# Memory stage: the final clips of six heads on POOL, two last-pass clips on DVE, another order

## The chip, the cores and the metric

The kernel runs on one core of a Trainium2 chip. The metric is the time of one execution on the device in microseconds (us), as a median over runs. The engines each have an instruction queue of their own, worked off in order: TensorE (PE) for matrix products, VectorE (DVE), ScalarE (ACT), GpSimd (POOL) and SyncE (SP), which issues transfers. They are tied together by semaphores.

## What is computed

A network of two layers on 4 x 512 rows of 256 numbers. Only the third of its four blocks, an attention over a memory of 256 vectors, is touched. It is repeated three times for each row and each of 8 heads, with entmax weights in place of a softmax:

```python
def entmax15(x):
    x = (x - jnp.max(x, -1, keepdims=True)) / 2.0
    xs = jnp.flip(jnp.sort(x, -1), -1)
    rho = jnp.arange(1, x.shape[-1] + 1, dtype=x.dtype)
    mean = jnp.cumsum(xs, -1) / rho
    meansq = jnp.cumsum(xs * xs, -1) / rho
    ss = rho * (meansq - jnp.square(mean))
    tau = mean - jnp.sqrt(jnp.clip((1.0 - ss) / rho, 0.0, None))
    support = jnp.sum(tau <= xs, -1, keepdims=True)
    tau_star = jnp.take_along_axis(tau, support - 1, -1)
    return jnp.square(jnp.clip(x - tau_star, 0.0, None))
...
for _ in range(NUM_STEPS):
    scores = jnp.einsum('bhsd,hnd->bhsn', xi, K) * beta
    w = entmax15(scores)
    xi = jnp.einsum('bhsn,hnd->bhsd', w, V)
out = xi.transpose(0, 2, 1, 3).reshape(B, S, H * hd) @ Wo.T
```

and then `x = x + layernorm(out)`.

## The kernel before

The rows stand in 16 tiles of 128 (one row per partition). A tile goes through three steps, so there are 48 units of work (`Unit`). Four tiles are in flight as four lanes: unit m is in lane m mod 4, and unit m+4 is the next step of the same tile, so its scores need the weights of unit m. The weight matrices are multiplied together beforehand into G1, G2 and G3.

A unit passes through these steps, each a small function of `memory_block`:

- PE: `score`, 16 matmuls into four PSUM banks (two heads, a pair, in each). The banks are shared by all units: pair p of a unit may be written once the first clip of that pair of the unit before has read it.
- DVE: `largest`, the eight largest scores of each head, eight instructions.
- A start value for the threshold: POOL `centre`, `square`, three `running_sum`, `mean_and_gap`, `mean_square`, `add_gap`, `add_room`; DVE `clear`; ACT `bound_root`; POOL `step_back`; DVE `bound`; POOL `start`, which writes `shift`. Each waits for the one before.
- Four Newton passes k = 0 to 3: ACT `clip`, relu(u + shift) for each of 8 heads, from PSUM into `u` in pass 0 and in place after that; DVE `take_moments`, one instruction per pair; DVE `invert`; POOL `second_moment`; ACT `newton_root`; POOL `newton`, which writes the next `shift`.
- `weights`, the final clip of each head with the last `shift`: before, all eight on DVE (line 1208).
- PE `transpose` (two heads at a time, with a warming matmul ahead), ACT `columns`, which squares the transposed weights into `wT`; after the third step PE `output`, DVE `out_stats`, POOL `out_rstd`, DVE `out_norm`.
- For the first step of a tile also DVE `tile_stats`, POOL `tile_rstd`, DVE `tile_rows`, PE `tile_transpose`, ACT `tile_columns`.

The `u` of three lanes lies in `mem_arena`, that of the fourth in `r_u`; rows of both names are the same work.

The order is written by hand for each engine as the body of a loop over slots n: a list of calls, each for the unit `Unit(n - something)`. One round of the loop, a slot, does one unit's worth of work on each engine, taken from several units at different steps. A call for a unit that isn't live issues nothing. Output and tile steps occur in 16 of the slots each; a slot with neither is called plain here.

Of the kernel before, what the change touches and what calls it, by code (L numbers as in the profile page):

```python
# [1046 lines left out]
DVE_HEADS = (0, 1, 2, 3, 4, 5, 6, 7)  # L1047
ACT_HEADS = ()
FIRST_SLOT, LAST_SLOT = -3, TILES * STEPS - 1 + 9
# [18 lines left out]
def memory_block(nc, T):  # L1068
    X, ident, vec, G1, G2, G3 = (T[n] for n in ("X", "ident", "vec", "G1", "G2", "G3"))
    col = lambda name, k: vec[:, VEC[name][0] + k:VEC[name][0] + k + 1]  # L1070
    with ExitStack() as ctx:
# [3 lines left out]
        def sem(name):  # L1075
# [49 lines left out]
        clipped, moments_ready, inv_ready, s2_ready, root_ready, shift_ready = (  # L1125
            [sem(f"{n}{k}") for k in range(PASSES)] for n in (
                "clipped", "moments_ready", "inv_ready", "s2_ready", "root_ready", "shift_ready"))
        dve_weights, act_weights, wT_in_psum, wT_ready = (sem(n) for n in (
            "dve_weights", "act_weights", "wT_in_psum", "wT_ready"))
# [16 lines left out]
        def _(dve):  # L1146
# [39 lines left out]

            def take_moments(a, k, *pairs):
                if not a.live:
                    return
                for p in pairs:  # L1190
                    dve.wait_ge(clipped[k], of_unit(a, NPAIR, p + 1))
                    last = dve.bn_stats(moments[:, a.lane, 2 * p:2 * p + 2, :].rearrange("p two c -> p (two c)"),  # L1192
                                        u[a.lane][:, 2 * p:2 * p + 2, :].rearrange("p two n -> p n two"))
                    if p == NPAIR - 1:
                        last.then_inc(moments_ready[k], 1)
# [29 lines left out]
            for n in range(FIRST_SLOT, LAST_SLOT + 1):  # L1225
                invert(Unit(n - 8), 3)
                largest(Unit(n - 5), 2)
                invert(Unit(n - 6), 0)
                largest(Unit(n - 5), 3)
                take_moments(Unit(n - 7), 2, 2, 3)  # L1230
                largest(Unit(n - 5), 4)
                weights(Unit(n - 8), 0)
                invert(Unit(n - 7), 2)
                largest(Unit(n - 5), 5, 6, 7)
                weights(Unit(n - 8), 1)
                take_moments(Unit(n - 6), 1, 0)
                weights(Unit(n - 8), 2)
                take_moments(Unit(n - 6), 1, 1, 2)
                take_moments(Unit(n - 7), 3, 0)
                weights(Unit(n - 8), 3)  # L1240
                take_moments(Unit(n - 6), 1, 3)
                take_moments(Unit(n - 7), 3, 1)
                clear(Unit(n - 5))
                weights(Unit(n - 8), 4, 5)
                invert(Unit(n - 6), 1)
                tile_rows(Unit(n - 2))
                take_moments(Unit(n - 7), 3, 2)
                bound(Unit(n - 5))
                weights(Unit(n - 8), 6, 7)
                take_moments(Unit(n - 7), 3, 3)  # L1250
                out_stats(Unit(n - 9))
                tile_stats(Unit(n + 3))
                take_moments(Unit(n - 6), 2, 0)
                take_moments(Unit(n - 5), 0, 0, 1, 2)
                out_norm(Unit(n - 9))
                take_moments(Unit(n - 5), 0, 3)
                take_moments(Unit(n - 6), 2, 1)
                largest(Unit(n - 4), 0, 1)

        @block.gpsimd  # L1260
        def _(pool):
# [100 lines left out]

            def out_rstd(a):
# [7 lines left out]
            for n in range(FIRST_SLOT, LAST_SLOT + 1):  # L1371
                running_sum(Unit(n - 5), 2)
                mean_and_gap(Unit(n - 5))
                mean_square(Unit(n - 5))
                add_gap(Unit(n - 5))
                add_room(Unit(n - 5))
                second_moment(Unit(n - 6), 1)
                step_back(Unit(n - 5))
                newton(Unit(n - 6), 1)
                start(Unit(n - 5))  # L1380
                out_rstd(Unit(n - 9))
                second_moment(Unit(n - 5), 0)
                tile_rstd(Unit(n - 1))
                second_moment(Unit(n - 7), 3)
                newton(Unit(n - 5), 0)
                newton(Unit(n - 7), 3)
                second_moment(Unit(n - 6), 2)
                newton(Unit(n - 6), 2)
                centre(Unit(n - 4))
                square(Unit(n - 4))  # L1390
                running_sum(Unit(n - 4), 0)
                running_sum(Unit(n - 4), 1)

        @block.scalar
        def _(act):
# [37 lines left out]
            def weights(a, *heads):  # L1433
                if not a.live:
                    return
                act.wait_ge(shift_ready[PASSES - 1], of_unit(a))
                for h in heads:
                    act.activation(u[a.lane][:, h, :], u[a.lane][:, h, :], ACT.Relu,
                                   bias=shift[:, a.lane, h:h + 1]).then_inc(act_weights, 1)

# [9 lines left out]
            for n in range(FIRST_SLOT, LAST_SLOT + 1):  # L1450
                clip(Unit(n - 3), 2, 0, 1)
                clip(Unit(n - 2), 0, 0, 1, 2, 3, 4, 5, 6, 7)
                clip(Unit(n - 3), 2, 2, 3)
                columns(Unit(n - 5), 2)
                clip(Unit(n - 3), 2, 4, 5)
                columns(Unit(n - 5), 3)
                newton_root(Unit(n - 2), 0)
                clip(Unit(n - 3), 2, 6, 7)
                newton_root(Unit(n - 4), 3)
                clip(Unit(n - 2), 1, 0, 1, 2)  # L1460
                tile_columns(Unit(n - 0))
                newton_root(Unit(n - 3), 2)
                clip(Unit(n - 2), 1, 3)
# [1134 lines left out]
```

## Time and profile before

| | us |
|---|---|
| median of 3 runs | 1927.84 |
| lowest, highest | 1927.65, 1935.23 |
| the profiled execution | 1928.65 |
| its span, first to last instruction | 1926.9 |

| engine | busy us | share of the span |
|---|---|---|
| PE, matmuls | 1657.8 | 86% |
| DVE | 1383.7 | 72% |
| ACT | 1166.3 | 61% |
| POOL | 611.3 | 32% |

The shares are means over stages. The page's strip of 40 slices shows the memory stage as the stretch in which DVE and ACT are at nine tenths or more, slices 12 to 27; POOL stands at four or five tenths there. Durations in rows run from the start of an instruction to its end; consecutive instructions of an engine overlap, so that what one costs its queue is the distance from its start to the next start.

### The profile page before, as it was taken

The numbers are of one execution on the slowest core, as the hardware profiler recorded it, in microseconds if no ns is written. First come the engines' busy times: TensorE is split into PE (matmuls) and PEld (weight loads), VectorE is DVE, ScalarE is ACT, GpSimd is POOL, SyncE is SP. The second block draws the span as 40 slices with busy tenths as digits, with TensorE's granted clock in tenths as the row PEclk, the third lists the DMA queues.
The fourth block names the chain that finished last, engine by engine and source line by source line (L and its number), as shares of the span: only waits on it lengthen the run. The fifth ranks groups of instructions, "written<-read, shape, count | busy, mean of one in ns | idle before, by whom it ended". The sixth has DMA issues, their size and how long they took to land. (4 is left out here: it accounts for less than half of the span.)

```text
span 1926.9 us, 26070 instructions
## 1 busy us (share of the span) xinstructions
PE 1657.8 (86%) x7634; PEld 1153.4 (60%) x7634; DVE 1383.7 (72%) x3597; ACT 1166.3 (61%) x2844; POOL 611.3 (32%) x1916
## 2 busy tenths in 40 slices
PE   5899999989657889988998789887688999999987
PEld 2545656465545667766786678665545556555554
DVE  6565747562359999999999999999444475665646
ACT  3242333311249999999999999999247364564640
POOL 3504224140034455545544555444210101002000
PEclk9698989998878889988998899889899999999989
DMA  5000000000300000000000000000000000000000
GB/s 217 1 1 1 1 1 1 0 1 1 118 1 1 1 1 1 1 1 1 1 1 1 1 1 1 1 1 1 1 1 1 1 2 1 1 12 0 8 6 22
DMA packets 6862, 19.90 MB, mean 10 GB/s; under 512 B 960, under 2 KB 3904, under 8 KB 5440
## 3 DMA queue, kind: packets, MB, share of 16 engines
q1 hardware_dynamic: 6720, 18.23, 2.5%
q8 instruction: 62, 1.02, 0.2%
q14 instruction: 80, 0.66, 0.1%
HBM read 16.13 MB, written 2.10 MB: 9 GB/s over the span
## 5 line engine op out<-in xcount | busy, mean ns | idle before, releaser
L1422 ACT ACTIVATE mem_arena<-mem_arena,r_shift 128x256 f32<-128x256 f32 x864 | 385.0, 510 | 23.1 <-POOL r_shift L1361 23.0
L1192 DVE BATCH_NORM_STATS2 r_moments<-mem_arena 128x6 f32<-128x512 f32 x576 | 380.4, 690 | 10.6 <-ACT mem_arena L1422 7.5
L1501 PE MATMUL r_bank<-G,r_wT 128*128 128x256 f32 x1024 | 234.7, 388 | 3.8 <-ACT mem_arena L1422 3.0
L1501 PEld LDWEIGHTS r_bank<-G,r_wT 128*128 128x128 f32 x1024 | 197.2, 196 | 35.1 <-issue 8.3
L1517 PE MATMUL r_bank<-ident,mem_arena 128*128 128x128 f32 x576 | 113.2, 330 | 73.2 <-DVE mem_arena L1208 73.1
L2047 ACT ACTIVATE e_rows_p<-e_seen,e_NM 128x512 f32<-128x512 f32 (+3 forms) x256 | 134.3, 557 | 64.1 <-DVE e_NM L1739 64.1
L1169 DVE MAX8 r_top<-r_bank 128x8 f32<-128x256 f32 x384 | 145.6, 406 | 19.4 <-PE r_bank L1501 19.0
L1511 PE MATMUL r_bank<-G,ident 128*128 128x256 f32 x384 | 143.6, 461 | 9.9 <-ACT r_wT L1448 9.7
L1517 PEld LDWEIGHTS r_bank<-ident,mem_arena 128*128 128x128 f32 x576 | 82.5, 169 | 115.8 <-DVE mem_arena L1208 106.7
L1501 PE MATMUL r_bank<-G,r_xnT 128*128 128x256 f32 x512 | 120.9, 397 | 24.4 <-ACT mem_arena L1422 23.7
L1739 DVE CUSTOM_DVE_ANT_0 e_seen<-e_banks,mask_q 128x512 f32<-128x512 f32 (+3 forms) x256 | 110.4, 486 | 43.3 <-PE e_banks L2250 42.2
L1192 DVE BATCH_NORM_STATS2 r_moments<-r_u 128x6 f32<-128x512 f32 x192 | 129.7, 691 | 8.9 <-ACT r_u L1422 8.2
L1422 ACT ACTIVATE r_u<-r_u,r_shift 128x256 f32<-128x256 f32 x288 | 131.8, 510 | 5.1 <-POOL r_shift L1361 5.1
L2058 ACT ACTIVATE mem_arena<-e_banks 128x512 f32<-128x512 f32 x160 | 92.4, 591 | 61.9 <-PE e_banks L2269 61.6
L1448 ACT ACTIVATE r_wT<-r_bank 128x512 f32<-128x512 f32 x192 | 116.6, 607 | 19.0 <-PE r_bank L1517 19.0
L1501 PEld LDWEIGHTS r_bank<-G,r_xnT 128*128 128x128 f32 x512 | 101.3, 201 | 40.3 <-issue 25.8
L1530 PE MATMUL r_bank<-G,r_wT 128*128 128x256 f32 x512 | 120.0, 384 | 4.8 <-DVE X L1223 4.8
L1422 ACT ACTIVATE mem_arena<-r_bank,r_shift 128x256 f32<-128x256 f32 x288 | 108.2, 483 | 1.3 <-POOL r_shift L1343 1.3
L1349 POOL TENSOR_TENSOR r_spread<-r_moments,r_inv_n 128x8 f32<-128x8 f32 x192 | 39.3, 205 | 212.1 <-DVE r_moments L1192 210.0
L1530 PEld LDWEIGHTS r_bank<-G,r_wT 128*128 128x128 f32 x512 | 95.8, 192 | 17.3 <-ACT r_wT L1448 5.4
L2269 PEld LDWEIGHTS e_banks<-ident,e_rows_p 128*128 128x128 f32 x640 | 74.2, 141 | 49.6 <-issue 25.0
L2269 PE MATMUL e_banks<-ident,e_rows_p 128*128 128x128 f32 x640 | 91.4, 274 | 6.8 <-ACT e_rows_p L2047 4.6
(295 smaller groups left out, 3308.2 us busy)
## 6 DMA issues: line engine op xcount, KB each, us to landing
w<-in_w SPq DMA_DIRECT2D x3, 1024.0 KB, 14.6
out_x<-X SPq DMA_DIRECT2D x4, 512.0 KB, 2.9
X<-in_x SPq DMA_DIRECT2D x1, 1536.0 KB, 10.8
w_in<-in_w_in SPq DMA_DIRECT2D x1, 1156.0 KB, 6.5
mem_arena<-in_wq SPq DMA_DIRECT2D x1, 1024.0 KB, 17.0
mem_arena<-in_wo SPq DMA_DIRECT2D x1, 1024.0 KB, 20.9
gate<-in_gate SPq DMA_DIRECT2D x1, 1024.0 KB, 6.5
up<-in_up SPq DMA_DIRECT2D x1, 1024.0 KB, 8.5
```

The lines of the kernel that those rows point to most:

```text
L1169: last = dve.max(top[:, a.lane, h, :], scores[:, h, :])
L1192: last = dve.bn_stats(moments[:, a.lane, 2 * p:2 * p + 2, :].rearrange("p two c -> p (two c)"), u[a.lane][:, 2 * p:2 * p + 2, :].rearrange ...
L1422: last = act.activation(u[a.lane][:, h, :], u[a.lane][:, h, :] if k else scores[:, h, :], ACT.Relu, bias=shift[:, a.lane, h:h + 1])
L1448: act.activation(wT[:, a.lane, 2 * p:2 * p + 2, :, :], bank[:, TB + p % 2, :], ACT.Square).then_inc(wT_ready, 1)
L1501: last = pe.matmul(scores[:, h, :], lhs, (G1 if a.first else G2)[:, h, i, :], start=i == 0, stop=i == 1)
L1511: pe.matmul(bank[:, TB + p % 2, 0:NMEM], ident[:], G1[:, 0, 0, :], start=True, stop=True)
L1517: last = pe.transpose(bank[:, TB + p % 2, i * P:(i + 1) * P], u[a.lane][:, h, piece * P:(piece + 1) * P], ident[:])
L1530: last = pe.matmul(bank[:, OUT, 0:D], wT[:, a.lane, h, piece, :], G3[:, h, piece, :], start=h == 0 and piece == 0, stop=h == NHM - 1 and p ...
L1739: last = dve.tensor_tensor_reduce(out=seen[:, j, c0:c0 + width], in0=bank[LOOK + j][:, c0:c0 + width], in1=T["mask_q"][:, S - width:], sca ...
L2047: last = act.activation(rows_p[:, j, P_AT[i]:P_AT[i] + width], seen[:, j, c0:c0 + width], ACT.Exp, scale=-1.0, bias=NM[:, i, j:j + 1])
L2058: act.activation(PT[kb][:, :, (i - kb) * P:(i - kb + 1) * P], bank[t_bank(a, g, r)].rearrange("p (j q) -> p j q", j=4), ACT.Copy).then_inc ...
L2269: last = pe.transpose(o[:, j * P:(j + 1) * P], rows_p[:, j, P_AT[i] + kb * P:P_AT[i] + (kb + 1) * P], ident[:])
```

## The change

`weights` of heads 2 to 7 moves from DVE to POOL, as a tensor_scalar with the same two operations; heads 0 and 1 stay on DVE. In the last pass (k = 3) the clips of heads 6 and 7 (pair 3) move from ACT to DVE, through a new function `clip` on DVE. PE waits for both sources of weights. The order lists of all four engines are rewritten, of which two lines stand here, and the loop begins two slots earlier.

```diff
-DVE_HEADS = (0, 1, 2, 3, 4, 5, 6, 7)
-ACT_HEADS = ()
-FIRST_SLOT, LAST_SLOT = -3, TILES * STEPS - 1 + 9
+DVE_HEADS = (0, 1)
+POOL_HEADS = (2, 3, 4, 5, 6, 7)
+DVE_CLIPS = ((), (), (), (3,))
+FIRST_SLOT, LAST_SLOT = -5, TILES * STEPS - 1 + 9
...
+            def clip(a, k, *heads):
+                if not a.live:
+                    return
+                dve.wait_ge(shift_ready[k - 1], of_unit(a))
+                for h in heads:
+                    last = dve.tensor_scalar(u[a.lane][:, h, :], u[a.lane][:, h, :], shift[:, a.lane, h:h + 1], 0.0,
+                                             ALU.add, ALU.max)
+                    if h % 2:
+                        last.then_inc(dve_clipped[k], 1)
...
                 for p in pairs:
-                    dve.wait_ge(clipped[k], of_unit(a, NPAIR, p + 1))
+                    if p in DVE_CLIPS[k]:
+                        dve.wait_ge(dve_clipped[k], of_unit(a, len(DVE_CLIPS[k]), DVE_CLIPS[k].index(p) + 1))
+                    else:
+                        dve.wait_ge(clipped[k], of_unit(a, NPAIR - len(DVE_CLIPS[k]), p + 1 - sum(q < p for q in DVE_CLIPS[k])))
...
+            def weights(a, *heads):
+                if not a.live:
+                    return
+                pool.wait_ge(shift_ready[PASSES - 1], of_unit(a))
+                for h in heads:
+                    pool.tensor_scalar(u[a.lane][:, h, :], u[a.lane][:, h, :], shift[:, a.lane, h:h + 1], 0.0, ALU.add,
+                                       ALU.max).then_inc(pool_weights, 1)
...
-                centre(Unit(n - 4))
-                square(Unit(n - 4))
+                centre(Unit(n + 2))
+                square(Unit(n + 2))
+                newton(Unit(n - 0), 2)
...
-                    pe.wait_ge(dve_weights, of_unit(a, len(DVE_HEADS), sum(h <= 2 * p + 1 for h in DVE_HEADS)))
-                    if any(h // 2 == p for h in ACT_HEADS):
-                        pe.wait_ge(act_weights, of_unit(a, len(ACT_HEADS), sum(h <= 2 * p + 1 for h in ACT_HEADS)))
+                    if any(h // 2 == p for h in DVE_HEADS):
+                        pe.wait_ge(dve_weights, of_unit(a, len(DVE_HEADS), sum(h <= 2 * p + 1 for h in DVE_HEADS)))
+                    if any(h // 2 == p for h in POOL_HEADS):
+                        pe.wait_ge(pool_weights, of_unit(a, len(POOL_HEADS), sum(h <= 2 * p + 1 for h in POOL_HEADS)))
```

DVE in the middle of the stage, before, from a unit's last three `largest` (MAX) through `clear` (TENSOR_SCALAR r_room) to the first instruction of its `bound`; L1192 is a moment, L1208 a weight clip, L1201 `invert`:

```order
L1169 MAX r_top<-r_bank 128x8 x3
L1208 TENSOR_SCALAR mem_arena<-mem_arena,r_shift 128x256
L1192 BN_STATS r_moments<-mem_arena 128x6
L1208 TENSOR_SCALAR mem_arena<-mem_arena,r_shift 128x256
L1192 BN_STATS r_moments<-mem_arena 128x6 x3
L1208 TENSOR_SCALAR mem_arena<-mem_arena,r_shift 128x256
L1192 BN_STATS r_moments<-mem_arena 128x6 x2
L1177 TENSOR_SCALAR r_room<-r_room 128x64
L1208 TENSOR_SCALAR mem_arena<-mem_arena,r_shift 128x256 x2
L1201 RECIPROCAL r_inv<-r_moments 128x8
L1192 BN_STATS r_moments<-mem_arena 128x6
L1183 TENSOR_TENSOR r_back<-r_back,r_fold 128x64
```

The same stretch of DVE in the changed kernel, in a plain slot too; L1206 is a moment, L1222 a weight clip, L1193 the new clip of the last pass:

```order
L1170 MAX r_top<-r_bank 128x8 x3
L1222 TENSOR_SCALAR r_u<-r_u,r_shift 128x256
L1215 RECIPROCAL r_inv<-r_moments 128x8
L1206 BN_STATS r_moments<-mem_arena 128x6
L1222 TENSOR_SCALAR r_u<-r_u,r_shift 128x256
L1206 BN_STATS r_moments<-mem_arena 128x6 x4
L1178 TENSOR_SCALAR r_room<-r_room 128x64
L1193 TENSOR_SCALAR mem_arena<-mem_arena,r_shift 128x256
L1206 BN_STATS r_moments<-mem_arena 128x6
L1184 TENSOR_TENSOR r_back<-r_back,r_fold 128x64
```

Between the last `largest` and `clear` there stand five moments, two weight clips and a reciprocal where there stood six moments and three weight clips; behind `clear` one weight clip and `invert` fewer.

POOL before, from a second moment and `newton` (L1358, L1361) to the three running sums (L1304), `centre` being L1287 and `square` L1295:

```order
L1349 TENSOR_TENSOR r_spread<-r_moments,r_inv_n 128x8
L1350 TENSOR_TENSOR r_meansq<-r_moments 128x8
L1352 TENSOR_TENSOR r_s<-r_spread,r_meansq 128x8
L1358 TENSOR_TENSOR r_spread<-r_root,r_s 128x8
L1361 TENSOR_TENSOR r_shift<-r_spread,r_inv 128x8
L1287 TENSOR_TENSOR r_fold<-r_top 128x8x8
L1295 TENSOR_TENSOR r_fold<-r_fold 128x8x8
L1304 TENSOR_TENSOR r_fold<-r_fold 128x16x8 x3
```

POOL in the changed kernel at the same place, from its fourth weight clip (L1381) on; L1371 and L1374 are `newton`, L1300 is `centre`, L1308 `square`, L1317 the sums:

```order
L1381 TENSOR_SCALAR r_u<-r_u,r_shift 128x256
L1371 TENSOR_TENSOR r_spread<-r_root,r_s 128x8
L1374 TENSOR_TENSOR r_shift<-r_spread,r_inv 128x8
L1381 TENSOR_SCALAR r_u<-r_u,r_shift 128x256 x2
L1362 TENSOR_TENSOR r_spread<-r_moments,r_inv_n 128x8
L1363 TENSOR_TENSOR r_meansq<-r_moments 128x8
L1365 TENSOR_TENSOR r_s<-r_spread,r_meansq 128x8
L1300 TENSOR_TENSOR r_fold<-r_top 128x8x8
L1308 TENSOR_TENSOR r_fold<-r_fold 128x8x8
L1371 TENSOR_TENSOR r_spread<-r_root,r_s 128x8
L1374 TENSOR_TENSOR r_shift<-r_spread,r_inv 128x8
L1317 TENSOR_TENSOR r_fold<-r_fold 128x16x8 x3
```

Weight clips now stand ahead of `centre`, and the `newton` of pass 2 stands between `square` and the sums.

## Rows read from the trace of the kernel before

**Rows 1.** Windows: stretch, us; busy (instructions) of PE, PEld, DVE, ACT, POOL; clock, DMA.

```profile
800.00:900.00 100.00, 82.03 (x357) 65.09 (x356) 97.01 (x251) 93.20 (x250) 50.07 (x200) 0.87 0.00 1
```

**Rows 2.** One line's instructions, `start`: duration least/median/most, first and last start.

```profile
L1343 POOL TENSOR_TENSOR r_shift<-r_neg,r_top x48: 208/246/248, 550.7 to 1330.8; 128x8 f32<-128x8 f32 x48
```

**Rows 3.** Groups by line, 700 to 1300 us: busy, mean ns, idle before, releaser.

```profile
L1422 ACT ACTIVATE mem_arena<-mem_arena,r_shift 128x256 f32<-128x256 f32 x650 | 290.1, 510 | 12.8 <-POOL r_shift L1361 12.7
...
L1349 POOL TENSOR_TENSOR r_spread<-r_moments,r_inv_n 128x8 f32<-128x8 f32 x144 | 29.4, 204 | 152.2 <-DVE r_moments L1192 150.7
...
L1221 DVE TENSOR_SCALAR r_onorm<-r_bank,r_omv,r_ors 128x256 f32<-128x256 f32 x12 | 6.4, 531 | 0.0
...
L1223 DVE TENSOR_TENSOR X<-X,r_onorm 128x256 f32<-128x256 f32 x12 | 5.1, 425 | 0.9
```

**Rows 4.** Timeline of DVE, 1077 to 1099 us: start, duration, instruction.

```profile
1081.85 0.18 DVE L1177 TENSOR_SCALAR r_room<-r_room 128x64 f32<-128x64 f32 x1
...
1083.15 0.20 DVE L1183 TENSOR_TENSOR r_back<-r_back,r_fold 128x64 f32<-128x64 f32 x1
...
1083.57 0.61 DVE L1208 TENSOR_SCALAR mem_arena<-mem_arena,r_shift 128x256 f32<-128x256 f32 x2
1084.09 0.69 DVE L1192 BATCH_NORM_STATS2 r_moments<-mem_arena 128x6 f32<-128x512 f32 x1
1084.70 0.69 DVE L1192 BATCH_NORM_STATS2 r_moments<-r_u 128x6 f32<-128x512 f32 x1
...
1089.40 0.18 DVE L1201 RECIPROCAL r_inv<-r_moments 128x8 f32<-128x8 f32 x1
1089.50 0.38 DVE L1169 MAX8 r_top<-r_bank 128x8 f32<-128x256 f32 x1
...
1092.10 1.14 DVE L1169 MAX8 r_top<-r_bank 128x8 f32<-128x256 f32 x3
1093.16 0.34 DVE L1208 TENSOR_SCALAR mem_arena<-mem_arena,r_shift 128x256 f32<-128x256 f32 x1
...
1096.33 0.34 DVE L1208 TENSOR_SCALAR mem_arena<-mem_arena,r_shift 128x256 f32<-128x256 f32 x1
```

**Rows 5.** Timeline of POOL over the same stretch.

```profile
1077.51 0.33 POOL L1287 TENSOR_TENSOR r_fold<-r_top 128x64 f32<-128x64 f32 x1
...
1081.34 0.32 POOL L1331 TENSOR_TENSOR r_room<-r_room,r_inv_k 128x64 f32<-128x64 f32 x1
1081.62 0.20 POOL L1349 TENSOR_TENSOR r_spread<-r_moments,r_inv_n 128x8 f32<-128x8 f32 x1
...
1082.12 0.23 POOL L1352 TENSOR_TENSOR r_s<-r_spread,r_meansq 128x8 f32<-128x8 f32 x1
...
1082.62 0.32 POOL L1337 TENSOR_TENSOR r_back<-r_mean,r_room 128x64 f32<-128x64 f32 x1 [0.27 <-ACT r_room L1412]
...
1091.12 0.20 POOL L1358 TENSOR_TENSOR r_spread<-r_root,r_s 128x8 f32<-128x8 f32 x1
1091.46 0.20 POOL L1361 TENSOR_TENSOR r_shift<-r_spread,r_inv 128x8 f32<-128x8 f32 x1
...
1093.32 0.32 POOL L1287 TENSOR_TENSOR r_fold<-r_top 128x64 f32<-128x64 f32 x1
...
1096.35 0.47 POOL L1319 TENSOR_TENSOR r_back<-r_mean 128x64 f32<-128x64 f32 x1
1096.89 0.32 POOL L1325 TENSOR_TENSOR r_room<-r_room,r_back 128x64 f32<-128x64 f32 x1
```

**Rows 6.** Groups by line and shape of POOL, whole span; columns as in rows 3.

```profile
L1304 POOL TENSOR_TENSOR r_fold<-r_fold 128x128 f32<-128x128 f32 x144 | 63.5, 441 | 11.3
...
L504 POOL TENSOR_TENSOR m_xd<-m_xt,m_dt 128x512 f32<-128x512 f32 x16 | 16.6, 1039 | 131.3 <-ACT m_xt L633 131.3
...
L1369 POOL TENSOR_TENSOR r_ors<-r_ove,half_neg 128x1 f32<-128x1 f32 x16 | 8.8, 549 | 2.6 <-issue 0.4
...
L1269 POOL MEMSET r_fold<- 128x256 f32 x3 | 0.8, 311 | 0.0
```

## What the change does to the time: the prediction

> **What bounds the kernel now.** I read the windows first: of 100 us of the memory stage DVE is busy 97.01 us, ACT 93.20, PE 82.03 and POOL 50.07 [rows 1]. So DVE is the bound, ACT follows closely, and POOL has room. The start instruction of the 48 units, one each, runs from 550.7 to 1330.8 us [rows 2]: 780.1 us over 47 intervals, 16.60 us per unit. The groups by line show that POOL's largest idle time is before the second moment: 152.2 us before 144 of them, four per unit, so 4.2 us per unit in which POOL waits for DVE's moments [rows 3].
>
> DVE's and POOL's timelines price the loop [rows 4, 5]. A slot without tile work runs from one `centre` at 1077.51 to the next at 1093.32: 15.81 us. It has two halves. In the first POOL makes the sums (last add 1081.34), DVE clears (1081.85), ACT takes the root, POOL steps back (1082.62) and DVE makes the bound (1083.15): 5.64 us. In the second DVE works through its queue from the bound to the end of the eighth `largest` (1092.10 plus 1.06, next instruction at 1093.16), and `centre` follows 0.16 us later: 10.17 us. In the first half DVE is never idle today, since moments and weights fill it; the loop and DVE's own load come out alike.
>
> **The change, engine by engine.** *DVE* loses six weight clips per unit and gains two clips of the last pass. Two clips took 0.52 us from start to next start (1083.57 to 1084.09), 0.26 each, so four fewer save 1.04 us. Its steady load falls from 97.01% of 16.60, 16.10, to 15.06 us. *ACT* loses two clips of 510 ns [rows 3]; from start to start they cost somewhat less, I take 0.4, so 0.8 us: from 15.5 to 14.7 us. *POOL* gains six tensor_scalar of 128x256. If nothing but load counted, a unit would take 15.06 plus today's 0.50 of DVE idle, 15.56 us, and the saving would be 1.04 times 48, 50 us.
>
> *The order.* It moves all four moments of pass 0 and of pass 2 ahead of the eighth `largest`, and leaves little between that and the clear. From the rows a moment costs 0.61 (1084.09 to 1084.70), a `largest` 0.35 (1.06 for three), a reciprocal 0.10 (1089.40 to 1089.50), the bound 0.42. Second half of the loop after the change: bound 0.42, one clip 0.26, ten moments 6.10, three reciprocals 0.30, eight `largest` 2.80, and 0.16 to `centre`: 10.04 us. The same sum for before (nine moments, three clips) is 9.95, against 10.17 in the trace. So this half is not shortened at all: one moment came in and two clips went.
>
> In the first half POOL's chain of sums cannot be hidden. Today it takes 3.83 us from `centre` to the last add. The new order puts a `newton` of pass 2 behind `square`: 0.34 (1091.12 to 1091.46) plus 0.16, of which about 0.1 hides in the wait for the square, so plus 0.4. DVE meanwhile has two weight clips, one reciprocal and five moments, 3.67 us, while the last add starts 0.16 plus 3.83 plus 0.4, 4.39 us, after the last `largest`, and its result comes 0.4 later. DVE will sit idle about 1.1 us in front of `clear` in every slot without tile work. What is queued behind: the clip of head 6, the moments and the bound, for which the next unit's first clips on ACT wait. Then clear 0.10, clip 0.26 and a moment 0.61 stand before the bound, 0.97 us, against 1.30 seen from clear to bound today. First half: 3.83 less some 0.1 (below), plus 0.4, plus 0.4 to the clear, plus 1.0: 5.5 us. The lower bound is 5.1 (the newton hidden whole), the upper 6.04 (3.83, 0.4, and the 0.51 and 1.30 of the trace), with the 0.22 by which the trace lay above my sum for the second half. Plain slot: 15.55 us, between 15.1 and 16.3, against 15.81 now. Where the last `largest` ends later than its load says, for a score that PE has late, that would add as well; PE's matmuls come in bursts with 18% idle [rows 1], and I count none.
>
> *Slots with tile work.* 16 of 48 slots hold an output norm. Its statistics and norm on DVE now lie in the idle stretch, but `out_rstd` on POOL stands before `add_gap`, and DVE's norm before `clear`. Counted from the last `largest`: POOL reaches `out_rstd` at 3.99 (the last add's 4.39 less one 0.40), takes 0.34 to its power (as from 1091.12 to 1091.46) and 0.55 for it [rows 6], then DVE's two norm instructions take 0.96 [rows 3]; with 0.1 for the hand-over the clear starts at 5.94 and not 4.79, 1.15 us later than in a plain slot. Tile statistics and rows, three instructions, become free. The tile's two columns on ACT stand just before the last-pass clip that DVE's moments wait for; I put this at 0.3 us in 16 slots. Mean: 15.55 + 1.15/3 + 0.3/3 = 16.03 us. Today's mean lies 0.79 above its plain slot, so part of the gain comes here.
>
> *POOL's clip.* No such instruction is in the trace. Nearest rows: a memset of the same 128x256 takes 311 ns, a tensor_tensor of 128x128 441, one of 128x512 1039 [rows 6]; on the line between these two 128x256 is 640. One input and one output lie between memset and tensor_tensor; I take 0.45, bounds 0.31 and 0.64, and as a further end 1.04, if halving the row saved nothing. POOL's budget between pass 3's moments and the next `centre` is the 7.8 us that DVE needs for eight moments, eight `largest` and one reciprocal. In it: three second moments of 0.66 (1081.62 to 1082.12, plus 0.16), two newtons of 0.5, a wait of some 0.9 for ACT's root, and six clips: 3.9 + 6w. It fits up to w = 0.65, just over my upper bound. At 0.45 all six are free.
>
> By the Trainium skill (GPSIMD Engine Reference, section 4.1) an elementwise instruction with one input runs there roughly at line rate, and its section 1 gives 1.2 GHz. Estimated from that page, 256 elements take 0.21 us, with the trace's 0.2 us for the smallest instructions some 0.42 us; the sum would stay what it is.
>
> *Contention.* Where a DVE clip began at 1096.33, POOL's 128x64 product took 0.47 us, and the next came 0.54 later rather than 0.40 [rows 5]: 0.14 us per meeting. The new order has two such clips in POOL's chain and not five, my 0.1 above; POOL's own clips meet DVE's moments and `largest` only. The Trainium skill (SBUF — State Buffer, section Who interferes with whom) says that a VectorE tensor_scalar in a two-port mode and a GpSimd instruction exclude each other for their whole length, and whichever starts later waits. By that rule a DVE clip that falls on a POOL clip would wait up to 0.45 us, with four per unit at most 1.8; by the order they don't meet.
>
> **Rivals.**
> 1. *Load alone decides*: DVE's idle is filled because `centre` or the sums come out earlier than I think. 15.56 us, 50 us saved, 1878. For it: DVE at 97%. Against it: the second half of the loop is DVE's own work and the first is serial.
> 2. *The upper ends hold*: plain slot 15.9 to 16.3, from ACT late at roots (it waits for `shift` of pass 2, now made after `square`) and more meetings. With 0.48 for tile work the mean is 16.4 to 16.8, and the time 1919 to 1937: no change that can be measured.
> 3. *POOL's clip is dear* (slower): above 0.65 us each clip delays `centre`, six times the excess per slot. It eats my 0.57 us at w = 0.75. At 0.9, near the middle of 0.64 and 1.04, the slot is 16.03 + 6 x 0.25 = 17.53 and the time 1928.65 + 47 x 0.93 = 1972. Against it: the one row with fewer than two inputs, the memset, lies at 0.31.
> The Trainium skill (GPSIMD Engine Reference, section 3.1) speaks against the change as a whole: "use DVE for elementwise". An estimate from the 2.6 cycles per element that it gives for two inputs is 0.55 us, with the trace's 0.2 for the smallest instructions 0.75, at which the change would bring nothing; no row here shows which rate holds for this form.
>
> **The numbers.** The sum is made on the profiled execution, 1928.65 us with a span of 1926.9; the median is 0.8 lower. 47 x (16.60 - 16.03) = 26.8 us; I let the filling and draining of the pipeline stand. 1928.65 - 26.8 - 0.8 = 1901; with a little for waits that no row shows, 1903. Chances: forecast (1890 to 1917) 0.5; load alone (below 1890) 0.14; upper ends 0.21; dear clip 0.15. For 8 in 10 the range goes from 1876 to 1936, with the forecast's own 1890 to 1917. A measurement of this kernel can tell 0.5%, 9.6 us, from no change. Faster by that: 0.65; within: 0.20; slower: 0.15.
>
> **What the new profile would show.** POOL tensor_scalar of 0.35 to 0.6 us; DVE idle about 1 us before `clear` in plain slots, ended by POOL; DVE busy 93 to 94% in the stage; starts about 16.0 apart. I am wrong if the clip is above 0.65 us, or if `clear` has no wait before it, or if ACT, which now idles 6.8 of 100 us [rows 1], shows over 12.

## The result

The changed kernel takes 2025.72 us (median of 4 runs, 2024.04 to 2030.28), before 1927.74 in the same comparison: ratio 1.050, interval 1.047 to 1.053. It is slower by 98 us where 25 us less were forecast.

All of it lies in the memory stage. The same row as in [rows 2] is, of the kernel after:

```profile
L1356 POOL TENSOR_TENSOR r_shift<-r_neg,r_top x48: 207/242/246, 551.0 to 1429.5; 128x8 f32<-128x8 f32 x48
```

878.5 us over 47 intervals make 18.69 us per unit, against 16.60 before. 47 times the difference is 98 us.

The windows of after, with the columns of [rows 1], show who is busy now:

```profile
800.00:900.00 100.00, 73.54 (x349) 61.04 (x347) 85.25 (x205) 79.49 (x210) 79.10 (x211) 0.93 0.00 1
```

DVE fell from 97 to 85, ACT from 93 to 79, and POOL rose from 50 to 79, so that no engine looks full. The reason is in two rows for POOL's new clip, of the view of one line's instructions (duration least/median/most):

```profile
L1381 POOL TENSOR_SCALAR mem_arena<-mem_arena,r_shift x216: 1134/1139/1247, 588.8 to 1455.8; 128x256 f32<-128x256 f32 x108
L1381 POOL TENSOR_SCALAR r_u<-r_u,r_shift x72: 1136/1139/1298, 643.2 to 1470.9; 128x256 f32<-128x256 f32 x72
```

1139 ns per head, where I had taken 450 and bounded at 640, with 1040 as a far end. Six of them are 6.8 us, added to POOL's serial work. POOL's timeline in one slot of after shows how they fill it up to `centre` (L1300):

```profile
1002.29 3.38 POOL L1381 TENSOR_SCALAR mem_arena<-mem_arena,r_shift 128x256 f32<-128x256 f32 x3
1005.64 0.20 POOL L1362 TENSOR_TENSOR r_spread<-r_moments,r_inv_n 128x8 f32<-128x8 f32 x1
...
1006.32 1.14 POOL L1381 TENSOR_SCALAR mem_arena<-mem_arena,r_shift 128x256 f32<-128x256 f32 x1
...
1007.95 2.36 POOL L1381 TENSOR_SCALAR mem_arena<-mem_arena,r_shift 128x256 f32<-128x256 f32 x2
1010.28 0.23 POOL L1362 TENSOR_TENSOR r_spread<-r_moments,r_inv_n 128x8 f32<-128x8 f32 x1
...
1010.97 0.29 POOL L1300 TENSOR_TENSOR r_fold<-r_top 128x64 f32<-128x64 f32 x1
```

The last two clips end at 1010.31. The second moment behind them starts without a wait, its moments being long there, and `centre` follows it without a wait, though DVE made its last `largest` of the unit by 1009.1 (1008.03 plus 1.08). From start to start a clip takes 1.12 us (3.38 less 1.14, halved).

Who waits for POOL, from the list of waits of after, 700 to 1300 us (total, times, longest):

```profile
ACT r_root L1455 <- POOL r_s L1365: 91.2, 64, 3.2
...
DVE r_moments L1206 <- ACT mem_arena L1446: 44.9, 84, 1.5
POOL r_spread L1362 <- DVE r_moments L1206: 30.9, 32, 1.6
```

ACT waits at the root for a second moment that stands in POOL's queue behind clips, for about 2.8 us per unit, and DVE waits for ACT's clips in turn. POOL's own wait for moments, 152 us in [rows 3], is down to 31.

### The profile page after: what moved, and what is told of

It is laid out like the page before. It is cut to its first block and busy times, and to the rows that moved or that the text cites. A ratio compares the mean times of both kernels' runs of the same rounds, so it can differ in the third digit from the quotient of the medians.

```text
span 2025.6 us, 26072 instructions
## 1 busy us (share of the span) xinstructions
PE 1669.5 (82%) x7634; PEld 1171.7 (58%) x7634; DVE 1358.1 (67%) x3405; ACT 1134.3 (56%) x2748; POOL 917.6 (45%) x2204
## 5 line engine op out<-in xcount | busy, mean ns | idle before, releaser
L1206 DVE BATCH_NORM_STATS2 r_moments<-mem_arena 128x6 f32<-128x512 f32 x576 | 386.1, 686 | 70.7 <-ACT mem_arena L1446 68.0
L1446 ACT ACTIVATE mem_arena<-mem_arena,r_shift 128x256 f32<-128x256 f32 x792 | 356.4, 506 | 26.6 <-POOL r_shift L1374 22.8
L1381 POOL TENSOR_SCALAR mem_arena<-mem_arena,r_shift 128x256 f32<-128x256 f32 x216 | 247.0, 1155 | 3.5
L1517 PEld LDWEIGHTS r_bank<-G,r_wT 128*128 128x128 f32 x1024 | 199.3, 198 | 54.4 <-ACT r_wT L1464 18.6
L1534 PEld LDWEIGHTS r_bank<-ident,mem_arena 128*128 128x128 f32 x576 | 93.2, 179 | 103.1 <-DVE mem_arena L1222 82.3
L1206 DVE BATCH_NORM_STATS2 r_moments<-r_u 128x6 f32<-128x512 f32 x192 | 129.7, 686 | 30.2 <-ACT r_u L1446 29.2
L1527 PEld LDWEIGHTS r_bank<-G,ident 128*128 128x128 f32 x384 | 74.8, 231 | 104.0 <-ACT r_wT L1464 101.4
L1446 ACT ACTIVATE r_u<-r_u,r_shift 128x256 f32<-128x256 f32 x264 | 120.2, 507 | 9.8 <-POOL r_shift L1374 8.5
L1455 ACT ACTIVATE r_root<-r_s 128x8 f32<-128x8 f32 x192 | 40.0, 208 | 142.5 <-POOL r_s L1365 142.5
L1446 ACT ACTIVATE mem_arena<-r_bank,r_shift 128x256 f32<-128x256 f32 x288 | 117.1, 490 | 1.3 <-POOL r_shift L1356 1.1
L1464 ACT ACTIVATE r_wT<-r_bank 128x512 f32<-128x512 f32 x192 | 108.9, 591 | 10.6 <-PE r_bank L1534 10.6
```

The source lines that it names most:

```text
L1381: pool.tensor_scalar(u[a.lane][:, h, :], u[a.lane][:, h, :], shift[:, a.lane, h:h + 1], 0.0, ALU.add, ALU.max).then_inc(pool_weights, 1)
L1446: last = act.activation(u[a.lane][:, h, :], u[a.lane][:, h, :] if k else scores[:, h, :], ACT.Relu, bias=shift[:, a.lane, h:h + 1])
L1464: act.activation(wT[:, a.lane, 2 * p:2 * p + 2, :, :], bank[:, TB + p % 2, :], ACT.Square).then_inc(wT_ready, 1)
L1517: last = pe.matmul(scores[:, h, :], lhs, (G1 if a.first else G2)[:, h, i, :], start=i == 0, stop=i == 1)
L1527: pe.matmul(bank[:, TB + p % 2, 0:NMEM], ident[:], G1[:, 0, 0, :], start=True, stop=True)
L1534: last = pe.transpose(bank[:, TB + p % 2, i * P:(i + 1) * P], u[a.lane][:, h, piece * P:(piece + 1) * P], ident[:])
```

## The experiments

**Theory A**: POOL's clip is dear by itself and pushes POOL's queue over a threshold of some 0.65 us per clip. **Theory B**: the new order costs the time, whatever a clip takes. **Theory C**: the clip is long only since it meets DVE's work.

### What POOL's forms cost alone

```diff
+            for n in (8, 64, 128, 256, 512):
+                four(n, lambda o, x: pool.tensor_scalar(o, x, col[:, 0:1], 0.0, ALU.add, ALU.max))
+            for n in (8, 256):
+                four(n, lambda o, x: pool.tensor_scalar(o, x, col[:, 0:1], None, ALU.add))
+            four(256, lambda o, x: pool.tensor_scalar(o, x, 1.0, 0.0, ALU.add, ALU.max))
+            four(256, lambda o, x: pool.tensor_scalar(o, x, 0.0, None, ALU.max))
+            four(256, lambda o, x: pool.tensor_copy(o, x))
+            four(256, lambda o, x: pool.tensor_tensor(o, x, src[:, 256:512], ALU.add))
+            four(256, lambda o, x: pool.tensor_tensor(o, x, col[:, 0:1].to_broadcast([P, 256]), ALU.add))
```

> The kernel before, with a stretch of its own between the memory and the experts stage in which POOL alone works, on scratch tiles: four each of tensor_scalar add+max with a per-partition scalar at 8, 64, 128, 256 and 512 columns, add alone at 8 and 256, add+max with constants at 256, max alone, copy, tensor_tensor and tensor_tensor with a broadcast column at 256. Theory A (the clip is dear by itself, per element): 1.1 us at 256, about 0.2 at 8, a straight line between, so some 0.67 at 128 and 2.1 at 512. Theory C (it is long since it meets DVE's work): under 0.7 at 256 with DVE silent. Whether the two operations or the per-partition scalar make the price is open; if each operation is a pass, add alone takes about 0.65. Time some 30 us over before.

The groups by line and shape of POOL (busy, mean ns of one):

```profile
L1566 POOL TENSOR_SCALAR q_dst<-q_src,q_col 128x512 f32<-128x512 f32 x4 | 7.9, 1992 | 0.2 <-issue 0.2
L1566 POOL TENSOR_SCALAR q_dst<-q_src,q_col 128x256 f32<-128x256 f32 x4 | 4.5, 1138 | 0.2 <-issue 0.2
L1569 POOL TENSOR_SCALAR q_dst<-q_src 128x256 f32<-128x256 f32 x4 | 4.2, 1066 | 0.2 <-issue 0.2
L1568 POOL TENSOR_SCALAR q_dst<-q_src,q_col 128x256 f32<-128x256 f32 x4 | 3.6, 928 | 0.2 <-issue 0.2
L1570 POOL TENSOR_SCALAR q_dst<-q_src 128x256 f32<-128x256 f32 x4 | 3.3, 846 | 0.2 <-issue 0.2
L1566 POOL TENSOR_SCALAR q_dst<-q_src,q_col 128x128 f32<-128x128 f32 x4 | 2.8, 712 | 0.2 <-issue 0.2
L1572 POOL TENSOR_TENSOR q_dst<-q_src 128x256 f32<-128x256 f32 x4 | 2.8, 722 | 0.1
L1573 POOL TENSOR_TENSOR q_dst<-q_src,q_col 128x256 f32<-128x256 f32 x4 | 2.3, 612 | 0.1
...
L1571 POOL COPY q_dst<-q_src 128x256 f32<-128x256 f32 x4 | 1.4, 398 | 0.1
L1566 POOL TENSOR_SCALAR q_dst<-q_src,q_col 128x8 f32<-128x8 f32 x4 | 1.2, 324 | 0.3 <-issue 0.3
```

The run, a single one, took 1973.45 us, 43 more than before beside it, for the stretch added, in which no other engine has an instruction. There the clip takes 1138 ns, as in the stage: theory C has fallen. It costs about 0.3 us plus 3.3 ns per column (1992 less 1138 over 256). It isn't two passes: the add alone takes 928, the max alone 846. It isn't the per-partition scalar: constants in its place take 1066. What is dear is the form. A tensor_tensor of the same size with its two inputs takes 722, and with the column broadcast 612. So the interpolation between tensor_tensor rows in my prediction, as a value for tensor_tensor, was fair (640 against 722); it was no bound for tensor_scalar. The Trainium skill (GPSIMD Engine Reference, section 4.1) gives one-input instructions as roughly line rate; the copy agrees with that (398 ns, where the estimate in the prediction was some 0.42 us), and no tensor_scalar of 256 columns here does: 846 at least.

### The changed kernel with a cheaper clip

```diff
-                    pool.tensor_scalar(u[a.lane][:, h, :], u[a.lane][:, h, :], shift[:, a.lane, h:h + 1], 0.0, ALU.add,
+                    pool.tensor_scalar(u[a.lane][:, h, 0:128], u[a.lane][:, h, 0:128], shift[:, a.lane, h:h + 1], 0.0, ALU.add,
```

> The changed kernel, but POOL clips only 128 of the 256 columns of each of its heads (the other half of the final clip is left out). Theory A (the price of POOL's clip, threshold 0.65 us): the clip takes about 0.67 us, slot 16.0 to 16.3, time 1900 to 1915. Theory B (the new order costs the time, whatever the clip takes): 1990 or more.

and the same with `0:64`:

> As the one with half the columns, but 64 of 256. Theory A: clip about 0.43 us, under the threshold with room, so POOL has slack and the time is that of the forecast, 1895 to 1910, hardly below the half-column run. Theory B: 1990 or more. If time falls in proportion to columns from the changed kernel through both, there is no threshold and my layout of POOL's budget is wrong.

| POOL's clips | ns of one | us, median | ratio to before | us per unit |
|---|---|---|---|---|
| six of 256 columns (the change) | 1139 | 2025.72 | 1.050 | 18.69 |
| six of 128 | 712 | 1914.04 | 0.992 (0.989 to 0.995) | 16.46 |
| six of 64 | 499 | 1908.56 | 0.990 (0.986 to 0.994) | 16.19 |

The column of units is the better measure: the memory stage is reached at 545.4 us (first `centre`) in the trace of the change, at 544.5 with 128 columns and at 553.9 with 64, through code that all three share. In 47 intervals 427 ns less bring 105 us, and the next 213 ns bring 13. That is a threshold, and theory B has fallen as the cause. Plain slots show it best, as the distance of two `centre` in POOL's timeline. The kernel after, then the one with 64 columns:

```profile
878.29 0.29 POOL L1300 TENSOR_TENSOR r_fold<-r_top 128x64 f32<-128x64 f32 x1
896.35 0.29 POOL L1300 TENSOR_TENSOR r_fold<-r_top 128x64 f32<-128x64 f32 x1
```

```profile
848.95 0.32 POOL L1300 TENSOR_TENSOR r_fold<-r_top 128x64 f32<-128x64 f32 x1 [0.40 <-DVE r_top L1170]
864.32 0.33 POOL L1300 TENSOR_TENSOR r_fold<-r_top 128x64 f32<-128x64 f32 x1 [0.29 <-DVE r_top L1170]
```

18.06 and 15.37 us. Under the threshold `centre` waits for DVE's `largest`; above it, it waits for nothing but its own queue. The difference divided by six clips is 0.45, so the threshold lies at 1.12 less 0.45, 0.67 us. Other plain slots of after take up to 18.28, which gives 0.63. With 128 columns, 0.69 us from start to start, the plain slots are at 15.69 and `centre` again has no wait: 0.32 us over six clips put the threshold at 0.64.

One thing moved beside the clips. The granted clock of TensorE from 700 to 1300 us is 0.92 before, 0.89 in after, and 0.98 and 0.99 in the two runs with cut clips. What part of the two runs' gain over before (0.8% and 1.0%) that is, no run separates; the threshold does not rest on it, since the plain slots end on DVE or on POOL.

### The order with all clips on DVE

```diff
-DVE_HEADS = (0, 1)
-POOL_HEADS = (2, 3, 4, 5, 6, 7)
+DVE_HEADS = (0, 1, 2, 3, 4, 5, 6, 7)
+POOL_HEADS = ()
...
-                weights(Unit(n - 8), 0)
+                weights(Unit(n - 8), 0, 1, 2, 3)
...
-                weights(Unit(n - 8), 1)
+                weights(Unit(n - 8), 4, 5, 6, 7)
```

> The changed kernel's order, but all eight final clips on DVE, heads 0 to 3 where head 0 stood and 4 to 7 where head 1 stood; POOL has none. Theory A: the six clips of 0.26 us go partly into DVE's idle 1.1 us before clear, slot 16.4 to 16.8, time 1918 to 1940, as before. Theory B: 1990 or more.

2024.59 us, ratio 1.051 (1.046 to 1.056): a miss for theory A as I had worked it out. With POOL free of clips the time is that of the change, for another reason. PE stands in the waits of this run, 700 to 1300 us:

```profile
POOL r_spread L1362 <- DVE r_moments L1206: 185.5, 114, 3.4
ACT r_room L1433 <- DVE r_room L1178: 51.0, 31, 2.5
...
DVE r_top L1170 <- PE r_bank L1514: 28.2, 38, 1.5
```

POOL waits for DVE, and DVE for scores and for its own longer queue before `clear`. As means over the units from 700 to 1300 us, `clear` starts 6.6 us behind `centre`, where it is 4.8 in the run with 64 columns, and from the bound to the end of the last `largest` it takes 11.2 us instead of 10.4. So about two thirds of the loss is DVE's own queue: I had counted on an idle time of 1.1 us there, six more clips need 1.56, and they take longer than 0.26 each beside POOL's sums. Here four of them take 1.43 us up to the next instruction at 867.54, though POOL has no clip in this run:

```profile
866.11 1.51 DVE L1222 TENSOR_SCALAR mem_arena<-mem_arena,r_shift 128x256 f32<-128x256 f32 x4
```

Most of the rest is waiting for scores, 0.9 us per unit against 0.1: PE must transpose a unit's eight heads before it makes the scores of four units on, so late clips lengthen a second loop, through PE. To test that, six of the eight clips were put ahead of the last three `largest` and two behind:

```diff
                 largest(Unit(n - 5), 2)
+                weights(Unit(n - 8), 0, 1)
...
                 largest(Unit(n - 5), 3)
+                weights(Unit(n - 8), 2, 3)
...
                 largest(Unit(n - 5), 4)
+                weights(Unit(n - 8), 4, 5)
...
                 largest(Unit(n - 5), 5, 6, 7)
-                weights(Unit(n - 8), 0)
+                weights(Unit(n - 8), 6, 7)
```

> All eight final clips on DVE in the new order, as in the run with heads 4 to 7 late, but six of them before the last largest and two right behind it, so that PE's transposes and with them its scores are not late. By the loop from bound to the last largest: six clips of 0.26 us are added to it, slot 16.2 + 1.6 = 17.8, time 1970 to 1985. If late transposes were not what made the other run slow, this one is at 2020 again.

1988.07 us, ratio 1.030 (1.025 to 1.035), 37 us less than the run with late clips and 3 us above the range given. It doesn't single out PE: the wait for scores fell by 0.5 us per unit, but `clear` is also back at 4.9 us behind `centre`, 1.7 less, and from the bound to the last `largest` it takes 1.0 more. Its plain slots:

```profile
887.36 0.32 POOL L1302 TENSOR_TENSOR r_fold<-r_top 128x64 f32<-128x64 f32 x1 [0.29 <-DVE r_top L1170]
904.44 0.33 POOL L1302 TENSOR_TENSOR r_fold<-r_top 128x64 f32<-128x64 f32 x1 [0.29 <-DVE r_top L1170]
```

17.08 us, 1.71 above the 15.37 with cheap clips on POOL, for six clips of 0.26 in the loop (1.56). So the order is fitted to clips that POOL makes; without them it is worse than the order before.

### Fewer heads on POOL

With four heads on POOL (4 to 7), 0 and 1 behind the last `largest`, 2 and 3 where head 1 stood:

```diff
-DVE_HEADS = (0, 1)
-POOL_HEADS = (2, 3, 4, 5, 6, 7)
+DVE_HEADS = (0, 1, 2, 3)
+POOL_HEADS = (4, 5, 6, 7)
...
-                weights(Unit(n - 8), 0)
+                weights(Unit(n - 8), 0, 1)
...
-                weights(Unit(n - 8), 1)
+                weights(Unit(n - 8), 2, 3)
```

> As the one with three, with four heads on POOL (4 to 7). By the threshold 3.9 + 4 x 1.12 = 8.4, 0.6 us over, slot 16.8, time 1928 to 1945. If the time falls evenly with the number of heads from the changed kernel's 2026: two heads fewer would be a third of the way to the forecast, 1985.

1941.58 us, ratio 1.006 (1.004 to 1.009), inside what the threshold gives and far from an even share per head; its ten runs spread from 1935 to 1954. Most plain slots are at 15.96, 0.59 over 15.37, and `centre` has no wait there: four clips of 1.12 are 0.6 too many, as 3.9 + 4w against 7.8 has it. With three heads, 5 to 7, and five on DVE (0, 1 and then 2, 3, 4 in the same two places):

> The changed kernel with three heads on POOL (5, 6, 7) and five on DVE. By the threshold: 3.9 + 3 x 1.12 = 7.3 us, under the 7.8 that DVE needs, so POOL is off the loop; the three clips more on DVE lie in its idle time before clear: slot 16.2 to 16.5, time 1908 to 1922. If the order is what costs: over 1960.

1964.67 us, ratio 1.017 (1.013 to 1.021): a miss. POOL was under its threshold (`centre` waits for `largest` again), but the clips don't fit in DVE's idle time before `clear`: it starts 5.5 us behind `centre`, 0.7 later than with 64 columns, and DVE's wait for scores grew by 0.3. In its list of waits ACT is idle for `clear`, and PE's scores wait for ACT's first clips, which free the banks:

```profile
PE r_bank L1516 <- ACT mem_arena L1445: 34.7, 17, 2.7
...
ACT r_room L1435 <- DVE r_room L1178: 28.2, 30, 2.1
```

Both were tried again with DVE's clips earlier. Four on POOL, 0 and 1 ahead of the last three `largest`, 2 and 3 behind them:

```diff
+                weights(Unit(n - 8), 0, 1)
                 largest(Unit(n - 5), 5, 6, 7)
-                weights(Unit(n - 8), 0)
+                weights(Unit(n - 8), 2, 3)
...
-                weights(Unit(n - 8), 1)
```

> The changed kernel with four heads on POOL (4 to 7) and four on DVE, heads 0 and 1 in front of the last three largest, 2 and 3 right behind them. Against the run with four heads and later clips (slots 16.0 to 18.8, 1942 us): POOL gets 0.5 us more room before centre, PE can transpose 0.6 us sooner. By the two-loop theory (POOL's budget in plain slots, PE's transposes, output and scores in output slots): plain 15.9 to 16.0, output slots 17.2 to 17.6, mean 16.4, time 1912 to 1928, so perhaps just below the kernel before. If PE has no part in it: 1938 to 1945 as there.

and three on POOL, 0 to 2 ahead and 3, 4 behind:

> The same with three heads on POOL (5 to 7), heads 0 to 2 in front of the last three largest, 3 and 4 behind. Two-loop theory: plain 15.38 + 3 x 0.26 = 16.2, output slots 17.3 to 17.7, time 1918 to 1932, against 1965 for the run with three heads and late clips. If the number of heads on POOL alone decided: 1965 again, or less than the run with four.

1951.86 us (ratio 1.011, 1.009 to 1.013) and 1960.90 (1.017, 1.014 to 1.019): two misses. With four heads some plain slots were as given, at 15.9 to 16.0, and others at 17.1 to 17.3. Once in twelve units DVE waits for scores for 3.4 to 3.6 us, which this row of its timeline shows in that run:

```profile
740.82 0.43 DVE L1170 MAX8 r_top<-r_bank 128x8 f32<-128x256 f32 x1 [3.36 <-PE r_bank L1517]
```

PE's timeline ahead of it, and the window of 732 to 736 us (columns as in [rows 1]):

```profile
726.42 0.60 PE L1527 MATMUL r_bank<-G,ident 128*128 128x256 f32 x2
...
730.81 1.22 PE L1527 MATMUL r_bank<-G,ident 128*128 128x256 f32 x2 [2.46 <-ACT r_wT L1464]
731.82 1.06 PE L1534 MATMUL r_bank<-ident,mem_arena 128*128 128x128 f32 x4
...
734.38 4.67 PE L1547 MATMUL r_bank<-G,r_wT 128*128 128x256 f32 x16
```

```profile
732.00:736.00 4.00, 4.00 (x15) 3.44 (x14) 3.49 (x9) 3.93 (x13) 1.75 (x9) 0.50 0.01 2
```

In the middle of the transposes PE waits 2.46 us for ACT's `columns` to free a bank, and behind that its granted clock is 0.50, the lower of its two levels (1.2 GHz). The warming matmul, 0.60 us before, takes 1.22, and the first half of the output 4.67 where the run with 64 columns has 3.62. The other two waits of over 3 us have the same wait of 2.46 and the same 0.50 ahead of them. Earlier weights on DVE thus let PE run into ACT's queue: it waits for `columns` for 58 and 66 us of 600 in these two runs, for 39 and 26 in those with later clips. `columns` earlier on ACT wasn't tried. No version of the new order with whole clips was faster than before.

### Two clips on POOL in the order before

```diff
-DVE_HEADS = (0, 1, 2, 3, 4, 5, 6, 7)
+DVE_HEADS = (0, 1, 2, 3, 4, 5)
+POOL_HEADS = (6, 7)
...
-                weights(Unit(n - 8), 6, 7)
...
                 start(Unit(n - 5))
+                weights(Unit(n - 8), 6, 7)
```

> The kernel before in its own order, with one thing moved: the final clips of heads 6 and 7 go from DVE (right behind bound) to POOL (right behind start), where POOL waits 4.4 us for moments. Two clips of 1.12 us fit in that wait, DVE loses 0.52 us per unit. If load on DVE decides there: up to 25 us saved, 1903 to 1918. Rival: the two clips end 2 us later, PE has the transposes of pair 3 in front of all scores of the next unit, and the scores then come late for DVE's largest: no gain or a loss, 1925 to 1960.

1979.45 us, ratio 1.024 (1.021 to 1.028), slower even than its rival gave. PE waits for the two clips, and DVE for the scores behind them:

```profile
DVE r_top L1170 <- PE r_bank L1502: 42.4, 50, 2.3
...
PEld r_bank L1519 <- POOL mem_arena L1368: 39.6, 22, 2.8
```

DVE's wait for scores is 1.3 us per unit where it was 0.1. POOL was idle at that place for 4 us, and yet the move costs 50 us: idle time on the engine that takes work over is not enough, the result has a reader.

### The last pass's clips back on ACT

```diff
-DVE_CLIPS = ((), (), (), (3,))
+DVE_CLIPS = ((), (), (), ())
...
-                clip(Unit(n - 7), 3, 6)
...
-                clip(Unit(n - 7), 3, 7)
...
-                clip(Unit(n - 5), 3, 5)
+                clip(Unit(n - 5), 3, 5, 6, 7)
```

> The changed kernel with the last pass's clips of heads 6 and 7 back on ACT, right behind head 5. Theory A (POOL's clips are the loop): 0.52 us less on DVE and 0.8 more on ACT change nothing, 2020 to 2035. If ACT was the second loop: over 2045.

2056.13 us, ratio 1.066 (1.062 to 1.069), 30 more than the change, and a miss for theory A, which had ACT out of the loop. 24 of the 30 us lie in the 47 intervals (19.20 us per unit against 18.69). POOL's queue holds a `newton` that waits for ACT's root, and this wait has grown; the changed kernel first, then this run, 700 to 1300 us:

```profile
POOL r_spread L1371 <- ACT r_root L1455: 14.1, 20, 0.8
```

```profile
POOL r_spread L1369 <- ACT r_root L1453: 28.3, 30, 1.4
```

14 us in some 32 units, 0.45 each; over 48 units that is 21 of the 24 us. Beside six clips on POOL this half of the change, DVE taking a pair of clips, is worth having; it was the other half that lost. What it brings without them no run shows.

### The output slots

In the run with 64 columns plain slots are at 15.4, but most of those with an output norm at 17.5. My forecast had 1.15 us for them. To see PE's share, half of the output product was left out there, pairs 0 and 1, which stand before the next scores:

```diff
-                    for i in range(4):
+                    for i in range(4 if p > 1 else 0):
                         h, piece = 2 * p + i // KN, i % KN
                         last = pe.matmul(bank[:, OUT, 0:D], wT[:, a.lane, h, piece, :], G3[:, h, piece, :],
-                                         start=h == 0 and piece == 0, stop=h == NHM - 1 and piece == KN - 1)
+                                         start=h == 4 and piece == 0, stop=h == NHM - 1 and piece == KN - 1)
```

> The run with a quarter of the columns, and of the output product only pairs 2 and 3 (PE's 16 half-matmuls of pairs 0 and 1, 3.6 us in front of the next scores, are left out). Theory PE (in output slots the next unit's scores wait behind output): the slots of 17.5 us fall to 16.3 to 16.8, time 1885 to 1895. Theory of my forecast (out_rstd and the norm before clear alone set the output slot): they stay at 17.5, time 1905 to 1912.

1893.44 us, 15 less, in the range of theory PE, but by luck. The slots of 17.5 fell only to 17.2, not to 16.3 to 16.8, and of the 15.5 us between the spans of the two profiled executions only 4.6 lie in the 47 intervals (16.09 us per unit against 16.19); the memory stage began 5.5 us earlier, and from the last `centre` to the end it took 5.5 less. So 3.6 us of PE's work are worth 0.35 us of an output slot, and theory PE fell as it stood. In the run with 64 columns, DVE just ahead of an output slot, and POOL in it:

```profile
937.07 0.43 DVE L1170 MAX8 r_top<-r_bank 128x8 f32<-128x256 f32 x1 [0.80 <-PE r_bank L1517]
```

```profile
943.09 0.32 POOL L1300 TENSOR_TENSOR r_fold<-r_top 128x64 f32<-128x64 f32 x1 [0.38 <-DVE r_top L1170]
...
947.10 0.56 POOL L1390 TENSOR_TENSOR r_ors<-r_ove,half_neg 128x1 f32<-128x1 f32 x1
```

DVE's norm starts at 947.70, 4.6 us after `centre`, and its two instructions keep `clear` back to 948.71, 5.62 us after `centre`, where a plain slot has 4.4: 1.2, the 1.15 us of the prediction. Three output slots from 700 to 1300 us have no tile columns on ACT in them. Two take 16.51 and 16.43 us, about 1.1 over the plain slot; the third takes 18.09, and 16.52 with half the output product left out, so that it is PE's. The slots at 17.5 all have those columns, for which I had 0.3 us; they cost 1.0 there. In the slot shown DVE waits 0.25 and 0.22 us for ACT's clips behind them, and 0.35 of the 1.0 went with half the output product. The slot before this one has columns and no norm and takes 17.12; the 0.80 before a `largest` is in it.

## Why the prediction was wrong

**The step that failed** is "One input and one output lie between memset and tensor_tensor; I take 0.45, bounds 0.31 and 0.64". It measured 1.14, 1.12 from start to start. I bounded a tensor_scalar by rows of other forms and let the count of inputs and outputs order them. The rows of POOL held no tensor_scalar at all, and nothing in them said that the forms rank so. The rival with the dear clip was there, with 0.15; by the rows it should have had more, since no row bounded the one price that could turn the sign. Two of the signs of being wrong came with it: the clip above 0.65 us, and ACT idle for 20.5 of 100 us. The third, no wait before `clear`, did not.

**What the rest of the working gives with the right price.** 3.9 + 6w against 7.8 put the threshold at 0.65; measured, 0.63 to 0.67. Rival 3's formula gives 16.03 + 6 x 0.47 = 18.85 us per unit at w = 1.12; measured, 18.69. The time, 1901 + 47 x 2.82 = 2034; measured, 2026. So the mechanism, POOL's budget between the moments of pass 3 and the next `centre`, was right, and a term was mis-sized. That the sum comes so close is in part luck: its base is 0.16 low (16.19 with 64 columns), and its excess 0.3 high, since the slots with a norm grew by only 2.2 us, from 17.4 to 19.6.

**Plain slots.** The slot that I priced, 1077.51 to 1093.32, has a `tile_rstd` on POOL, so it is not without tile work; late in the stage slots with none take 15.75 and 15.82, and some 16.3 to 16.6, so the price stands as that of the short ones. Forecast 15.55 us, bounds 15.1 and 16.3; with the clip under the threshold 15.37. The serial chain through `centre`, sums and `clear` limits the unit there, as worked out, and not DVE's load of 15.06 with its idle time kept. DVE's wait before `clear` is there, 0.73 us where I had 1.1, in a plain slot of the run with 64 columns:

```profile
853.35 0.20 DVE L1178 TENSOR_SCALAR r_room<-r_room 128x64 f32<-128x64 f32 x1 [0.73 <-POOL r_room L1344]
```

**Slots with tile work.** 1.15 and 0.3 us were the forecast; the mean came out 0.82 above the plain slot (16.19 less 15.37) where I had 0.48. The norm's 1.15 was right (16.43 and 16.51 in slots with the norm and no columns, the one of 18.09 aside). The 0.3 for the tile's columns on ACT was the small term: such slots take 17.5 with a norm and 17.1 without. PE, which I had counted as idle enough, is the other: 0.35 us of the slots at 17.5, the 0.80 before a `largest` ahead of them, and most of the slot of 18.09.

**Had the clip cost 0.45**, the run with 64 columns (0.50) says about what would have come: 1908.6, against 1903 forecast. Only its columns left out were cheaper; the rest of its work is that of the change. The steps to it were less good than the number: its 47 intervals save 19 us and not 27, the stage began 9 us late in the profiled execution, and from the last `centre` to the end it took 8.5 us less than before, the draining that I had let stand.

**Contention.** DVE's weight clips took 341 ns on average before, 401 beside POOL's long clips, with a longest of 580, and 338 with clips of 64 columns: 0.06 us twice per unit, a small sum, as forecast. It isn't proper to POOL's clip: in the run with all clips late on DVE they took 425 on average, up to 585, beside POOL's sums. The Trainium skill (SBUF — State Buffer, section Who interferes with whom) has the later one wait for the other's end. The run with four heads and earlier clips doesn't bear that out for this pair. Here POOL's clip lasts to 866.70, and two DVE clips that start 0.33 us behind it are through in 0.60, no longer than two without it [rows 4]:

```profile
865.51 1.19 POOL L1381 TENSOR_SCALAR mem_arena<-mem_arena,r_shift 128x256 f32<-128x256 f32 x1
```

```profile
865.84 0.60 DVE L1222 TENSOR_SCALAR mem_arena<-mem_arena,r_shift 128x256 f32<-128x256 f32 x2
```

In that run 73 DVE clips lie wholly inside a POOL clip, with a mean of 357 ns and a longest of 569. So there is a price per meeting, of at most some 0.24 us, and not a wait for the other's whole length.

**ACT and DVE's pair.** I gave the pair moved from ACT to DVE a cost and a gain by load, 0.52 and 0.8 us. Its gain is real, 24 us in the stage, but as latency before a root, which POOL waits for.

## What to carry to other kernels

Price an instruction by its form on its engine, and where the trace has no row of that form, measure it alone before an order is built around it: here four instructions in an idle stretch would have told the sign. An order built on a wrong price is fitted to that price; the same order was 1% faster than before with a clip of 0.5 us and 5% slower with the real one. An engine that takes over work must have idle time and its readers must be able to wait; each queue behind the result is another loop, and those of PE and of ACT's `columns` were the ones that I left out.

## What the runs showed of the hardware

On POOL tensor_scalar costs about 0.3 us plus 3.3 ns per column with two operations (324 ns at 8 columns, 712 at 128, 1138 at 256, 1992 at 512), more than a tensor_tensor with two full inputs (722 at 256). On DVE the same clip takes 0.26 us from start to start, so POOL is 4.3 times slower for this form, and 1.7 times for a form that one would compare it by (a tensor_tensor add of 128x256 on POOL, 722 ns, against DVE's 425 in [rows 3]). The price hardly changed with the work of other engines: a median of 1139 ns in the stage, 1298 at most.

TensorE's matmuls took about twice as long behind a wait of 2.46 us, at a granted clock of 0.50: 1.22 us for a warming matmul where it had been 0.60.
